# Forty-three stages at other steps in a hand-planned Perceiver kernel on one NeuronCore

## The reference

```python
for l in range(6):
    x = attention(x, None,    ..., causal=True,  attn_bias=bias, freqs=freqs) + x   # 128 keys, one null key
    x = attention(x, context, ..., causal=False, attn_bias=None, freqs=None) + x    # 2048 keys, one null key
    x = feedforward(x, ff_norm_g[l], ff_w1[l], ff_w2[l]) + x                        # 128 -> 2 x 512 -> 128
out = layernorm(x, final_g, stable=True) @ proj_w
# attention(): 16 heads of 64; q and k are l2-normed; one key/value head shared by all query heads
# the cell, for each step: c = sigmoid(..c..) * c + sigmoid(..c..) * tanh(..c..)
```

## Time and profile before

| | |
|---|---|
| median of 3 runs | 2848.99 us (2847.93 to 2850.33) |
| the profiled execution | 2856.2 us, of which its span 2854.5 us |
| busy: TensorE / VectorE / ScalarE / GpSimd | 2560.8 / 2355.5 / 2068.4 / 608.1 us |
| mean granted TensorE clock | 0.956 of 2.4 GHz |
| first window | 0 to 98.7 us |
| window of run 0's core | 98.7 to 202.8 us |
| 22 windows of the loop | 202.8 to 2622.6 us |
| last core with `t`, then `u`, then `v` | 2622.6 to 2854.5 us |

### The profile page before, as it was taken

How to read it: one execution, slowest core, us unless ns; L and a number is a source line. 1 busy time by engine, 2 the same in 40 slices (tenths; PEclk the granted TensorE clock), 3 DMA queues, 4 the chain that set the end, 5 groups by cost and what they waited for, 6 DMA issues and landing times.

```text
span 2854.5 us, 44143 instructions
## 1 busy us (share of the span) xinstructions
PE 2560.8 (90%) x12652; PEld 1551.9 (54%) x12652; DVE 2355.5 (83%) x4427; ACT 2068.4 (72%) x3861; POOL 608.1 (21%) x392
## 2 busy tenths in 40 slices
PE   4799999999998998998999999999999999999876
PEld 2455555555555555555555555555555555555555
DVE  6689888888888888888887888887888888888875
ACT  2577877777777777878777777777787777787531
POOL 2312312312212213213113123122122131130000
PEclk7799999999999999999999999999999999999886
DMA  3000010000000001001001001001001001000000
GB/s 118 23 8 16 23 34 16 23 28 16 23 23 27 23 1 43 9 15 49 8 15 43 8 16 49 8 16 43 8 16 49 3 21 29 15 8 24 1 1 4
DMA packets 16661, 64.43 MB, mean 23 GB/s; under 512 B 2241, under 2 KB 7410, under 8 KB 11642
## 3 DMA queue, kind: packets, MB, share of 16 engines
q1 hardware_dynamic: 16378, 61.13, 6.8%
HBM read 48.25 MB, written 0.29 MB: 17 GB/s over the span
## 4 chain that ended last, share of the span: by engine, by line
PE 43%; DVE 21%; issue 17%; POOL 10%; ACT 8%; DVEq 0%; ACTq 0%; DMA 0%; SPq 0%; POOLq 0%
PE psS L1054 11%; PE psO L1102 6%; POOL rn L424 6%; PE psO L1105 5%; PE psO L1103 5%; DVE PL L638 5%; POOL qs_all L465 4%; ACT P L892 3%; DVE rows_sb L617 2%; DVE ss L572 2%; DVE rows_sb L609 2%; PE psL L1159 2%; ACT PH L889 2%; PE psL L1047 2%; DVE oTs L622 2%
## 5 line engine op out<-in xcount | busy, mean ns | idle before, releaser
L638 DVE TENSOR_TENSOR PL<-P,PH 128x512 fp32r<-128x512 f32 x1536 | 1124.9, 759 | 119.4 <-ACT P L892 72.4
L889 ACT ACTIVATE PH<-psS 128x512 fp32r<-128x512 f32 x1536 | 945.6, 616 | 227.5 <-PE psS L1054 201.6
L892 ACT ACTIVATE P<-psS 128x512 f32<-128x512 f32 x1536 | 950.7, 619 | 37.4 <-DVE PL L638 37.2
L1054 PE MATMUL psS<-QT,KT 128*128 128x512 f16 x3072 | 941.3, 390 | 0.7 <-ACT P L892 0.7
L1102 PE MATMUL psO<-PH,V 128*128 128x512 f32 x1536 | 891.6, 580 | 0.0
L1105 PE MATMUL psO<-PL,V 128*128 128x512 f32 x1536 | 613.8, 400 | 0.0
L1103 PE MATMUL psO<-PH,VL 128*64 128x512 f32 x1536 | 613.3, 399 | 0.0
L1054 PEld LDWEIGHTS psS<-QT,KT 128*128 128x128 f16 x3072 | 217.9, 100 | 348.2 <-issue 261.0
L1102 PEld LDWEIGHTS psO<-PH,V 128*128 128x128 f32 x1536 | 297.8, 194 | 184.1 <-issue 15.6
L1105 PEld LDWEIGHTS psO<-PL,V 128*128 128x128 f32 x1536 | 293.5, 191 | 155.7 <-issue 7.4
L424 POOL TENSOR_TENSOR rn<-ssc,neghalf 128x16 f32<-128x16 f32 (+2 forms) x73 | 235.8, 3230 | 355.0 <-DVE ssc L573 302.1
(11 more groups left out here) (365 smaller groups left out, 2908.3 us busy)
## 6 DMA issues: line engine op xcount, KB each, us to landing
ctx_sb<-ctxT SPq DMA_DIRECT2D x24, 1024.0 KB, 4.8
KT<-KT SPq DMA_DIRECT2D x48, 256.0 KB, 3.7
W<-wpack SPq DMA_DIRECT2D x6, 1280.0 KB, 6.3
W<-wpack SPq DMA_DIRECT2D x6, 1088.0 KB, 7.1
W<-wpack SPq DMA_DIRECT2D x6, 576.0 KB, 6.4
KT<-biasM SPq DMA_DIRECT2D x1, 1024.0 KB
W<-tail_w SPq DMA_DIRECT2D x1, 832.0 KB
P<-biasW SPq DMA_DIRECT2D x1, 512.0 KB
```

Of the source, the lines that this page charges most:

```text
L638: nc_v.tensor_tensor(PL[:, here, :], P[:, t % PSLOTS, :], PH[:, here, :], ALU.subtract).then_inc(sem("p_lo"), 1)
L889: nc_a.activation(PH[:, t % HSLOTS, :], bank, ACT.Exp, scale=SIM_SCALE).then_inc(sem("p_hi"), 1)
L892: nc_a.activation(P[:, t % PSLOTS, :], bank, ACT.Exp, scale=SIM_SCALE).then_inc(sem("ca_exp"), 1)
L1054: ins = mm(bank, keys[part], q, start=(part == 0), stop=(part == 1))
```

## The change

The four tables get new steps for 43 of 361 entries; nothing else changes, and every stage does what it did. The lines behind the tables stand four lower in the changed file (L889 is L885 there).

In every window of the loop these move: `f_raw_sa` (ACT 3 to 4), `f_kraw2` (ACT 14 to 13) and `f_kraw3` (13 to 14), `f_khi` (ACT 22 to 24), `f_turn_q_sa` (PE 15 to 16), `e_scale1` (DVE 40 to 41), `b_down` (PE 56 to 59) and `b_end` (DVE 62 to 64). In the first window `s_bias` (DVE 2 to 1), `s_table` (PE 11, ACT 12, DVE 11, all to 10) and `s_ready` (DVE 22 to 20). The rest are 30 entries of `u` stages. Since no core runs in their window, only the order within a queue counts there: on PE `b_up` comes before `u_turn1`; on DVE `u_key2` before `b_silu`, `u_cell1` behind `u_mask3`, `u_sum2` and `u_back1`, `u_sum3` behind `u_back3`, and `b_end` before `u_z`; ACT and POOL keep their order.

```diff
 PLAN_PE
-            15: ["f_turn_q_sa", "u_turn_y2", "t0_turn_y2"], 16: ["t0_qkv"], 18: ["b_turn", "u_qkv"],
+            15: ["u_turn_y2", "t0_turn_y2"], 16: ["f_turn_q_sa", "t0_qkv"], 18: ["b_turn", "u_qkv"],
...
 PLAN_ACT
-            3: ["f_raw_sa"], 4: ["f_raw_sa2"], 7: ["f_kraw0"], 8: ["f_sq_sa"], 10: ["f_kraw1"], 12: ["s_table"],
-            13: ["f_hi_sa", "f_kraw3"], 14: ["f_kraw2"], 15: ["f_ksq"], 17: ["f_QT_sa"], 20: ["b_tanh"],
-            22: ["u_gates0", "f_sne", "f_se0", "t0_exp0", "f_khi"], 23: ["f_se1"], 24: ["u_exp0"], 25: ["t0_exp1"],
+            4: ["f_raw_sa", "f_raw_sa2"], 7: ["f_kraw0"], 8: ["f_sq_sa"], 10: ["f_kraw1", "s_table"],
+            13: ["f_hi_sa", "f_kraw2"], 14: ["f_kraw3"], 15: ["f_ksq"], 17: ["f_QT_sa"], 20: ["b_tanh"],
+            22: ["f_sne", "f_se0", "t0_exp0"], 23: ["f_se1", "u_gates0"], 24: ["u_exp0", "f_khi", "u_exp1"], 25: ["t0_exp1"],
...
 PLAN_DVE
-            0: ["f_begin", "f_norm_sa"], 1: ["e_null", "f_xnT_sa"], 2: ["s_bias", "s_null"], 3: ["b_spread3"],
+            0: ["f_begin", "f_norm_sa"], 1: ["e_null", "s_bias", "f_xnT_sa"], 2: ["s_null"], 3: ["b_spread3"],
```

More of the change, by code:

```diff
@@ L266, in build @@
         PLAN_ACT = {
-            3: ["f_raw_sa"], 4: ["f_raw_sa2"], 7: ["f_kraw0"], 8: ["f_sq_sa"], 10: ["f_kraw1"], 12: ["s_table"],
-            13: ["f_hi_sa", "f_kraw3"], 14: ["f_kraw2"], 15: ["f_ksq"], 17: ["f_QT_sa"], 20: ["b_tanh"],
[4 rows of a table removed]
-            59: ["f_hi_ca"], 62: ["f_QT_ca"],
-            65: ["v_gates2", "v_exp0", "v_exp1", "v_exp2", "v_exp3", "v_back0", "v_back2", "v_gates3"],
+            4: ["f_raw_sa", "f_raw_sa2"], 7: ["f_kraw0"], 8: ["f_sq_sa"], 10: ["f_kraw1", "s_table"],
+            13: ["f_hi_sa", "f_kraw2"], 14: ["f_kraw3"], 15: ["f_ksq"], 17: ["f_QT_sa"], 20: ["b_tanh"],
[3 rows of a table added]
@@ L275, in build @@
+            41: ["t1_back0"], 45: ["t1_back2"], 52: ["f_raw_ca"], 53: ["f_sq_ca"], 54: ["f_KT"], 59: ["f_hi_ca"],
+            62: ["f_QT_ca"], 65: ["v_gates2", "v_exp0", "v_exp1", "v_exp2", "v_exp3", "v_back0", "v_back2", "v_gates3"],
         }
         PLAN_DVE = {
-            0: ["f_begin", "f_norm_sa"], 1: ["e_null", "f_xnT_sa"], 2: ["s_bias", "s_null"], 3: ["b_spread3"],
+            0: ["f_begin", "f_norm_sa"], 1: ["e_null", "s_bias", "f_xnT_sa"], 2: ["s_null"], 3: ["b_spread3"],
             4: ["b_invert3"], 5: ["b_widen3"], 6: ["f_V0", "f_V1"], 7: ["b_scale3", "t0_largest", "u_largest"],
-            9: ["f_ss_sa", "t0_final", "u_final"], 10: ["s_turned"], 11: ["f_V2", "f_unit_sa", "t0_in", "s_table"],
+            9: ["f_ss_sa", "t0_final", "u_final"], 10: ["s_turned", "s_table"], 11: ["f_V2", "f_unit_sa", "t0_in"],
@@ L280, in build @@
             12: ["f_V3", "u_in"], 13: ["t0_norm", "t0_gain"], 14: ["b_out", "f_kss", "u_norm"], 15: ["t0_own"],
             16: ["b_xnT", "u_gain", "t1_largest"], 17: ["f_null", "t0_key0"], 18: ["f_kunit", "t0_key1", "t1_final"],
[9 rows of a table removed]
[7 rows of a table added]
             33: ["b_act", "f_widen1", "t0_back1", "t1_key2", "t1_mask1"], 34: ["f_scale1", "t1_key3"], 35: ["t1_mask2"],
[3 rows of a table removed]
[3 rows of a table added]
             45: ["f_widen3", "t0_cols"], 46: ["f_scale3"], 47: ["t1_back3"], 48: ["f_out", "t0_res"], 49: ["f_xnT_ca"],
-            50: ["u_out", "s_rows"], 51: ["t0_z"], 54: ["e_spread2", "e_invert2", "f_ss_ca", "f_KT"],
@@ L297, in build @@
-            55: ["u_cols", "e_widen2"], 57: ["t1_out", "u_res", "f_unit_ca"], 58: ["u_z"],
-            59: ["t1_cols", "t1_res", "e_scale2"], 60: ["f_nv"], 61: ["t1_z"], 62: ["b_end"],
[2 rows of a table added]
+            61: ["t1_z"], 64: ["b_end", "u_z"],
             65: ["v_largest", "v_final", "v_in", "v_norm", "v_gain", "v_own", "v_key0", "v_key1", "v_cell2", "v_mask0", "v_key2", "v_mask1", "v_key3", "v_mask2", "v_sum0", "v_mask3", "v_sum1", "v_sum2", "v_sum3", "v_back1", "v_back3", "v_out", "v_cols", "v_res", "v_z", "v_cell3"],
@@ L304, in build @@
             21: ["t1_y2"], 30: ["f_out"], 37: ["f_ca"], 38: ["s_rows"], 40: ["f_ca_q"], 49: ["f_low_ca"], 54: ["t0_z"],
-            56: ["t1_z"], 57: ["u_z"], 65: ["v_fin", "v_y", "v_y2", "v_z"],
+            56: ["t1_z"], 60: ["u_z"], 65: ["v_fin", "v_y", "v_y2", "v_z"],
         }
```

## The result

| | before | changed |
|---|---|---|
| median | 2848.46 us (2846.97 to 2850.33, 4 runs) | 2810.27 us (2807.40 to 2813.38, 4 runs) |
| ratio | | 0.987, 95% interval 0.9855 to 0.9884 |
| span of the profiled execution | 2854.5 us | 2808.6 us |
| mean granted TensorE clock in it | 0.956 | 0.971 |
| first window / window of run 0's core | 98.7 / 104.1 us | 98.9 / 99.0 us |

The account below looks back on a forecast made before the run. It took a VectorE chain up to `f_sk2` as the bound. 23 windows gave 35.7 us, clock 7.7, with +1.6 and -3 once: -44.8 us, median 2849.0 to 2804 us, range 2780 to 2843.

Parts of the forecast that it names:

- The bound: Each loop window: a chain through VectorE up to `f_sk2` sets the time, so what VectorE saves before it shortens the window.
- `f_raw_sa`, -0.55 us a window: ScalarE copy one step later: fills idle time, second copy starts 0.57 us earlier, norms follow; bounds 0 to -1.0.
- `f_turn_q_sa`, the two waits: TensorE query turn one step later: wait of 3.39 becomes 1.7 us, back rows' 0.32 about 1.5; by itself gains 0.
- Its clock term, a third of 23 us: Splitting TensorE's idle stretch at the query turn avoids some clock falls: -0.35 us a window, bounds 0 to -1.05.
- `f_khi`, -1.0: ScalarE step 22 to 24: key's low half on GpSimd no longer stops VectorE's `Psn` or `Ps`; bounds +0.4 to -1.5.
- The rival in which the low half wins the pair: GpSimd beats VectorE's `PL` at 1019.35, margin 0.2 us, so `f_khi` gives 0: 2827 us, chance 0.20.
- Edits at nothing: `f_kraw2`/`f_kraw3` swapped, `e_scale1`, `b_down` and `b_end` later: 0 us, as nobody waits for the last two in the window.
- First window, +1.6: Once: `s_table` ahead of `f_V2` and `f_unit_sa` on VectorE delays the self-attention chain; bounds 0 to +3 us.
- `u`, -3 (0 to -4): Window of `u`, once: `u_cell1` behind `u_mask3` brings last exponential, turn and sums 2.9 us earlier; `b_end` goes into a wait.
- The falls twice: TensorE steps 16 to 19: a clock fall after each of two waits, up to +19 us, 2868 us, chance 0.10.

## Why the prediction held, step by step

- **The bound** (a chain through VectorE up to `f_sk2`) held. `f_khi` and `f_raw_sa` alone bring `f_sk2` forward; `f_turn_q_sa` alone leaves the chain where it was. TensorE's next wait for VectorE, at L1159 before the self-attention's output projection, is 1.27 us in the window read and 1.25 in the changed kernel, so VectorE still sets the time there.
- **`f_raw_sa`, -0.55 us a window**: 0.4 in the chain. The step from the earlier copy to the reduce was taken as one to one; the reduce stands behind VectorE's own queue, which gave back a quarter. The edit alone is worth 17 us all the same, the rest by the clock as far as the means tell; the prediction put the clock's share down to `f_turn_q_sa` only.
- **`f_turn_q_sa`, the two waits**: 1.7 and 1.5 forecast, 1.86 and 1.46 measured. **Its clock term, a third of 23 us**, was too small. All 15 falls at this place are gone, and alone it is worth 18 us, in the company of the others 11. The argument for a third was a fall behind a wait of 2 us at L1061. It says little on this place: in the changed kernel none of the waits of 1.4 to 2.2 us at L1057 was followed by a fall. By the rule of the Trainium skill that the text weighed ("TensorE: Matmul & The Clock Gate", Part 1) the whole would go, and the trace agrees at waits of 1.86 and 1.46; at 2.23 eight windows still fell.
- **`f_khi`, -1.0**: 1.4 to 1.5. The order came out as described, with `Psn` and both `Ps` at their own length; the window read was of the cheaper kind. In 15 of the 22 windows it was a `Ps` that lost 1.94 us, for which the prediction had 1.4, and the term took the 1.0 of the other seven. These 15 are the very windows whose clock falls at the turn: behind the fall the key's low half comes at least 0.6 us later (44.4 us into the window instead of 43.8) and meets a `Ps` instead of `Psn`. The rival in which the low half wins the pair did not come: in the window shown `PL` starts at 458.44, 0.2 us ahead of it as worked out, and the low half takes 2.47 us where it took 2.14.
- **Edits at nothing: the step that failed.** "No DMA is moved on SP" and "`b_down` ...: nobody waits for them in the window" are wrong. The queue's instructions kept their order, but one of them waits for `b_down`, and the swap is behind it. That costs 22 to 25 us, by three kernels, over half as much as the change gained in all: without it the ratio is 0.9782, 2785 us, 62 us faster than before. The other edits at nothing (`f_kraw2` and `f_kraw3`, `e_scale1`) and those of the first window were not run alone.
- **First window, +1.6**: +0.2 in the trace, within its bounds. The window of run 0's core, which was counted with 1.55 us, got 5.1 shorter; its clock fell for 6.8 us before and not at all in the changed kernel. **`u`, -3 (0 to -4)**: 5.4, above its bounds, by the copy described.
- **The falls twice** (the slower rival) did not happen: no window has a fall at that place.

So the forecast of -44.8 came near -38.2 partly by luck, by two errors of opposite sign: without the late swap the change gives 62 us, some 17 more than the terms, mostly by `f_khi` and the clock, and the late swap takes 24 back. The single edits alone add up to more (34 + 17 + 18 + 5 = 74 us), so they overlap, and the share of each in the 62 is not shown but for `f_khi` (35, taken out) and `f_turn_q_sa` (11, taken out).

## What to carry to other kernels

A stage that is moved releases more than its engine's neighbours: look up who waits for its semaphore on the DMA queue, and what stands behind that wait there, for a transfer that the next stage needs may be held up by a load that nobody needs yet. Give such a queue the order in which its transfers are needed, not the order in which it was convenient to write them. Before moving work ahead on one engine, find what the next engine's queue has in front of the step that is to gain: a reduce moved past one product gave 10 us, projections moved past a product that someone waited for cost 30.

## What was not expected of the hardware

- A VectorE instruction with one SBUF input can be stopped by GpSimd as well: `back_x<-xs` (128x128 float32, SBUF to SBUF) took 2.28 us beside the low half, in all 22 windows of the loop, and 0.21 to 0.23 otherwise. The prediction counted only products of two SBUF tiles. The Trainium skill, "SBUF — State Buffer", Who interferes with whom, names `tensor_scalar` among the operations that can take the shared pair; the trace agrees.
- The second half of the swap of KT took 7.75 us from issue to landing behind the two weight loads and 3.7 us ahead of them.
- Waits at which the clock fell were not told apart by their length alone: one of 2.23 us was followed by a fall in 8 of 22 windows and not in the other 14, and one of 1.86 by none in three kernels and by one in the fourth.
